# A grouped feed-forward moved into its layer's causal attention, its router behind the first unit, and weights laid out ahead

## The chip, the cores and the metric

One NeuronCore of a Trainium2 chip runs the whole program in one launch. The metric is device time in microseconds (us) of one execution. Two times are close enough to be called the same when they differ by less than about half a per cent.

## The reference

Four layers work on x, 2 sequences of 1024 tokens of 128 channels. In each, the normalized input goes both to an attention and to a feed-forward, and the layer's output joins the two (the feed-forward's result, after an activation, here silu, multiplies the attention's before it is added to the input). The layers: linear attention and a capacity mixture of experts; near (relative) attention and a ternary feed-forward; rotary causal attention and a grouped mixture; biased causal attention and a clamped mixture. Each attention has 16 heads of 8 channels (the first has 64).

The third layer's feed-forward, cut to its core:

```python
scores = sigmoid(x @ w_gate.T)                      # 16 experts, in 4 groups
group_scores = top_k(scores.reshape(T, 4, 4), 2)[0].sum(-1)
allowed = the 2 best groups;  idx = the 4 best experts among them
w = scores[idx] / (scores[idx].sum(-1) + 1e-6)
y = sum over experts of w * ((silu(x @ w1.T) * (x @ w3.T)) @ w2.T)   # F = 64 each
  + the same with the shared expert (F = 128) and no gate
```

All tokens go through all experts and are weighted: 16 experts of 64 rows make 8 blocks of 128, the shared one a ninth. Everything is float32.

## The kernel before

Channels or tokens lie on 128 partitions; the 2048 tokens are 4 chunks of 512. Program parts ("phases") follow one another, each with a block per engine: the prologue of a layer's attention (`a2j`: joins the layer before, normalizes, projects q, k, v), the attention (`a2a`), its output projection (`a2o`), the feed-forward (`f2`). The names of the fourth layer are `a3j`, `a3a`, `a3o` and `f3`.

`causal_attention` (L2149) goes through 8 units, each one sequence and 4 heads. A unit's first pass has 20 jobs ("max"): TensorE writes scores (bf16, split into parts) into one of two "rooms" of 128x1024 in PSUM (L2450, masks L2457), and VectorE takes row maxima from it (L2333). After half of the tokens the maxima are split into three bf16 parts, turned by TensorE (job "maxima", L2462), cast (L2358) and stored by DMA into the stacks as further rows (L2403). The second pass has 40 steps ("st"): scores again, less the maxima, transposed, into one of three PSUM banks (L2481, masks L2488); ScalarE takes exp (L2422); and 12 "pv" steps multiply with the values (L2500, float32). After half of a unit ScalarE copies the result (L2429), and a job "context" turns it in a room (L2469), where VectorE divides it (L2369, L2372).

TensorE takes its work in a list that `work_order` (L2191) writes ahead by a model of costs and due times: at each point the first pass's next job or the second pass's next step, whichever it expects to be able to start sooner. The orders of ScalarE (`act_order`) and of the SyncE DMA queue (`dma_order`) follow from that list. SyncE first loads the next unit's stacks, then the weights of the layer's feed-forward and of the next prologue (`after`), then takes rows and loads in that order, and last stores the gates.

Behind all first passes come the router's jobs, in the same rooms (`GroupRouter`, L1087): four "weight" jobs turn 25 blocks of the feed-forward's weights (L1117) and VectorE copies them out (L1128); logits (L1036); then a chain on VectorE (L1133 to L1164), with one exp on ScalarE (L1045), that chooses groups and experts; two jobs that turn the gates (L1050, copies L1054). While that runs, TensorE has what is left of the second pass.

`grouped_ffn` (L1240) then has 36 steps (4 chunks, 9 blocks): two products 128x512 into PSUM (L1268, L1271), silu (L1295), their product (L1314), that times the gate rows (L1319; two DMAs per step bring a gate row to 64 partitions each), and the down product, which adds up over the 9 blocks (L1282). The shared block has no gate (L1308). ScalarE takes the chunk's silu into `gT` (L1288). Everywhere in it up runs two steps ahead of down.

Of the kernel before, what the change touches and what calls it, by code (L numbers as in the profile page):

```python
# [20 lines left out]
ALU = mybir.AluOpType  # L21
# [3 lines left out]
P = 128  # L25
BATCH = 2
# [183 lines left out]
def linear_weights(nc, ph, w):  # L210
    H, DH, F = 16, 64, 32
    PAIRS = H * DH // P
    wq, wk, wv = (ph.sb(n, [P, H * DH]) for n in ("wq", "wk", "wv"))
# [5 lines left out]
    pairs = [(wq[:], w["Wq"]), (wk[:], w["Wk"]), (bq[:], columns(w["bq"])), (bk[:], columns(w["bk"])),  # L219
# [4 lines left out]
    return (wq, wk, wv, wproj, bq, bk, bv, bproj, featq, featk), pairs  # L224


class Features:
# [5 lines left out]
    def __init__(self, nc, k, ph, tiles, out):  # L233
        self.nc, self.k = nc, k
        self.wq, self.wk, self.bq, self.bk, self.featq, self.featk = [tiles[i] for i in (0, 1, 4, 5, 8, 9)]
        self.wqf, self.wkf, self.bqf, self.bkf = out
        self.wT = [ph.sb(name, [P, self.PAIRS, DIM]) for name in ("wqT", "wkT")]
        self.turn, self.prod = [ph.ps(f"turn{i}") for i in range(2)], [ph.ps(f"prod{i}") for i in range(4)]
        self.key_bias = ph.sb("key_bias", [P, self.PAIRS, self.FP])
        self.turned, self.copied, self.multiplied, self.biased = ph.sem("turned"), ph.sem("copied"), ph.sem("multiplied"), ph.sem("biased")  # L240

    def weights(self, pe):

        lots = [(i, h) for i in range(2) for h in range(2)]
        for n in range(len(lots) + 1):
            if n < len(lots):
                i, h = lots[n]
                if n >= 2:
                    pe.wait_ge(self.copied, n - 1)
                for g in range(4):  # L250
                    mm = self.nc.tensor.transpose(self.turn[n % 2][:, g * P:(g + 1) * P],
                                                  (self.wq, self.wk)[i][:, (4 * h + g) * P:(4 * h + g + 1) * P], self.k.ident[:])
                mm.then_inc(self.turned, 1)
            if n:
                i, h = lots[n - 1]
                pe.wait_ge(self.copied, n)
                for g in range(4 * h, 4 * h + 4):
                    mm = self.nc.tensor.matmul(self.prod[i][:, g * self.FP:(g + 1) * self.FP], self.wT[i][:, g, :],
                                               (self.featq, self.featk)[i][:], start=True, stop=True)
                if h:  # L260
                    mm.then_inc(self.multiplied, 1)
# [801 lines left out]
class GateRows:  # L1063
# [11 lines left out]
    def load(self, sp, m, srcs, hid_ready, read_by):  # L1075

        if m >= self.KEPT:
            sp.wait_ge(hid_ready, read_by)
# [366 lines left out]
H = 16  # L1445
# [1775 lines left out]
```

## Time and profile before

| | us |
|---|---|
| median of 3 runs | 1858.84 (1857.61 to 1865.55) |
| the profiled execution | 1859.92 |
| its span, first to last instruction | 1858.0 |
| TensorE busy | 1544.7 (83%) |
| VectorE busy | 1175.6 (63%) |
| ScalarE busy | 918.5 (49%) |
| GpSimd busy | 478.4 (26%) |
| mean granted TensorE clock | 0.903 |

Where the stages of the third layer lie, in us from the span's start:

| stage | from | to |
|---|---|---|
| prologue a2j | 879 | 931 |
| attention a2a, first passes | 931 | 1156 |
| attention a2a, rest of the second passes | 1156 | 1225.5 |
| projection a2o | 1225.7 | 1233.8 |
| feed-forward f2 | 1234 | 1327.4 |
| fourth layer's prologue a3j | 1327.9 | 1371 |

Engines: PE is TensorE, PEld its weight loads, DVE VectorE, ACT ScalarE, POOL GpSimd, SP SyncE with its DMA queue. PE's ends are modelled, so that consecutive matmuls overlap in their listed durations; a busy TensorE isn't one at its peak. "PEclk" is the clock granted to TensorE as a share of 2.4 GHz. L12 is line 12 of the kernel before.

### The profile page before, as it was taken

The numbers are of one execution on the slowest core, as the hardware profiler recorded it, in microseconds if no ns is written. First come the engines' busy times: TensorE is split into PE (matmuls) and PEld (weight loads), VectorE is DVE, ScalarE is ACT, GpSimd is POOL, SyncE is SP. The second block draws the span as 40 slices with busy tenths as digits, with TensorE's granted clock in tenths as the row PEclk, the third lists the DMA queues.
The fourth block names the chain that finished last, engine by engine and source line by source line (L and its number), as shares of the span: only waits on it lengthen the run. The fifth ranks groups of instructions, "written<-read, shape, count | busy, mean of one in ns | idle before, by whom it ended". The sixth has DMA issues, their size and how long they took to land. (4 is left out here: it accounts for less than half of the span.)

```text
span 1858.0 us, 32947 instructions
## 1 busy us (share of the span) xinstructions
PE 1544.7 (83%) x12129; PEld 746.3 (40%) x12129; DVE 1175.6 (63%) x2514; ACT 918.5 (49%) x1765; POOL 478.4 (26%) x416
## 2 busy tenths in 40 slices
PE   5979745998888888888569988899838988889997
PEld 4656522334343443434224444344323343344443
DVE  4324667755765675805668888435657888617777
ACT  2332232666666666674226666432214666554443
POOL 0702447756766665720300000000020100000000
PEclk9989765999999999999759999689867999889999
DMA  7232257666766766610430100023170010004332
GB/s 213 86 92 72 54 167 196 177 161 163 191 170 163 197 155 167 175 39 9 128 85 19 37 20 19 1 66 91 37 222 16 23 36 19 2 4 104 101 99 82
DMA packets 225671, 179.15 MB, mean 96 GB/s; under 512 B 59536, under 2 KB 194120, under 8 KB 225352
## 3 DMA queue, kind: packets, MB, share of 16 engines
q1 hardware_dynamic: 215400, 160.34, 32.6%
q10 hardware_dynamic: 8064, 12.51, 2.3%
q0 software_dynamic: 2048, 4.20, 0.8%
q8 instruction: 97, 1.59, 0.4%
q14 instruction: 62, 0.51, 0.1%
HBM read 108.64 MB, written 67.64 MB: 95 GB/s over the span
## 5 line engine op out<-in xcount | busy, mean ns | idle before, releaser
L1981 DVE TENSOR_REDUCE a1a_partial<-a1a_room 128x4 f32<-128x1024 f32 x192 | 226.4, 1220 | 30.9 <-PE a1a_room L2046 30.2
L2422 ACT ACTIVATE a3a_probsT<-a3a_st 128x512 f32<-128x512 f32 (+2 forms) x320 | 155.6, 560 | 129.5 <-PE a3a_st L2488 79.2
L2422 ACT ACTIVATE a2a_probsT<-a2a_st 128x512 f32<-128x512 f32 (+2 forms) x320 | 155.5, 560 | 129.5 <-PE a2a_st L2488 77.2
L1940 ACT ACTIVATE a1a_probsT<-a1a_st 128x512 f32<-128x512 f32 (+1 forms) x416 | 204.7, 575 | 11.8 <-PE a1a_st L2079 10.5
L2333 DVE TENSOR_REDUCE a3a_maxima<-a3a_room 128x2 f32<-128x1024 f32 (+3 forms) x160 | 170.1, 1112 | 38.2 <-PE a3a_room L2457 24.9
L2333 DVE TENSOR_REDUCE a2a_maxima<-a2a_room 128x2 f32<-128x1024 f32 (+3 forms) x160 | 170.1, 1112 | 28.4 <-PE a2a_room L2457 19.7
L1845 POOL TENSOR_TENSOR a1a_shifted<-a1a_shifted,a1a_best 128x1024 f32<-128x1024 f32 x64 | 121.8, 1904 | 91.0 <-DVE a1a_best L1987 64.7
L2116 PE MATMUL a1a_ctx<-a1a_probsT,a1a_vpad 128*9 128x512 f32 (+3 forms) x1408 | 139.0, 493 | 0.8
L1977 DVE CUSTOM_DVE_ANT_0 a1a_shifted<-a1a_room,a1a_bands 128x256 f32<-128x256 f32 x256 | 93.3, 421 | 73.3 <-PE a1a_room L2046 65.6
L2046 PE MATMUL a1a_room<-stack 48*128 48x128 bf16 (+1 forms) x1376 | 108.4, 261 | 35.8 <-DVE a1a_partial L1981 19.5
L2079 PE MATMUL a1a_st<-stack 51*128 51x512 bf16 (+3 forms) x576 | 116.3, 314 | 19.9 <-ACT a1a_nearT L1947 6.4
L1943 ACT ACTIVATE a1a_probsT<-a1a_st 128x512 f32<-128x512 f32 x128 | 73.4, 603 | 114.0 <-PE a1a_st L2088 114.0
L2382 POOL COPY a_vpad<-a_values 128x256 f32<-128x256 f32 x16 | 6.3, 401 | 428.0 <-PE a3a_ctx L2500 211.8
L2481 PE MATMUL a3a_st<-stack 51*128 51x512 bf16 (+3 forms) x384 | 87.7, 352 | 18.5 <-DMA stack<-a3a_parts 9.4
L2481 PE MATMUL a2a_st<-stack 51*128 51x512 bf16 (+3 forms) x384 | 89.3, 357 | 14.2 <-ACT a2a_probsT L2422 7.8
L2500 PE MATMUL a3a_ctx<-a3a_probsT,a_vpad 128*32 128x512 f32 (+3 forms) x768 | 90.5, 549 | 7.7 <-ACT a3a_probsT L2422 4.7
L2500 PE MATMUL a2a_ctx<-a2a_probsT,a_vpad 128*32 128x512 f32 (+3 forms) x768 | 92.5, 560 | 4.0 <-ACT a2a_ctxT L2429 2.0
L2046 PEld LDWEIGHTS a1a_room<-stack 48*128 48x128 bf16 x1376 | 46.6, 99 | 117.9 <-DVE a1a_partial L1981 62.1
L2450 PE MATMUL a3a_room<-stack 48*128 48x512 bf16 (+3 forms) x384 | 68.0, 356 | 25.0 <-DMA stack<-k 14.4
L2450 PE MATMUL a2a_room<-stack 48*128 48x512 bf16 (+3 forms) x384 | 67.7, 354 | 25.1 <-PEq L2570 15.9
L1400 ACT ACTIVATE f_below<-f_a,r_r_gate_room 128x512 f32<-128x512 f32 x64 | 44.0, 687 | 85.7 <-PE f_a L1374 85.6
L1857 POOL TENSOR_TENSOR a1a_beyond<-a1a_probsT,c_beyond_mask 128x512 f32<-128x512 f32 x56 | 70.9, 1272 | 56.3 <-ACT a1a_probsT L1943 56.3
(491 smaller groups left out, 3139.0 us busy)
## 6 DMA issues: line engine op xcount, KB each, us to landing
a1a_bands<-a_band SPq DMA_DIRECT2D x112, 192.0 KB, 4.0
a_near<-a1a_shifted SPq DMA_DIRECT2D x112, 192.0 KB, 3.1
a1a_near<-a_near SPq DMA_DIRECT2D x64, 256.0 KB, 4.3
f_rows<-l_gates SPq DMA_DIRECT2D x64, 256.0 KB, 3.1
a_band<-a1a_r_mix SPq DMA_DIRECT2D x64, 254.0 KB, 3.7
stack<-q SPq DMA_DIRECT2D x96, 96.0 KB
f_rows<-l_gates SPq DMA_DIRECT2D x64, 128.0 KB, 3.1
stack<-k SPq DMA_DIRECT2D x32, 96.0 KB
```

Of the source, the lines that this page charges most:

```text
L1845: nc.gpsimd.tensor_tensor(shifted[:, V % 2, t], shifted[:, V % 2, t], best[:, V % 2, :, t:t + 1].broadcast_to([P, HG, NEAR]), ALU.subtract ...
L1940: nc.scalar.activation(dst, src, ACT.Exp).then_inc(exp_done, 1)
L1977: ins = nc.vector.tensor_tensor_reduce(shifted[:, V % 2, t, place, :], src[:, place // 2, place % 2, :], band[i][:, place, :], 1.0, LOWEST ...
L1981: nc.vector.tensor_reduce(partial[:, g % 2, :, 1 + r].rearrange("p (a s) -> p a s", a=2), src, X_AXIS, ALU.max).then_inc(job_free, 1)
L2046: mm = nc.tensor.matmul(dst[:, lo + i * P:lo + (i + count) * P], q, rows_of(sides[edge], place, STACK)[:, c * P:(c + count) * P], start=Tr ...
L2079: mm = nc.tensor.matmul(dst[:, to:to + count * P], rows_of(sides[edge], place + j, ALL_ROWS)[:, c * P:(c + 1) * P], query_rows(q_stack, pl ...
L2116: mm = nc.tensor.matmul(ctx[32 * h:32 * h + DH + 1, lo * P:hi * P], vpad[b][right][:, c, h, :], probsT[:, block_index(V, at) % BLOCK_ROOMS ...
L2333: nc.vector.tensor_reduce(best, scores, X_AXIS, ALU.max).then_inc(job_free, 1)
L2422: nc.scalar.activation(probsT[:, block_at % BLOCK_ROOMS, place:place + heads, lo:], src, ACT.Exp).then_inc(exp_done, 1)
L2450: mm = nc.tensor.matmul(dst[:, end - width:end], query_rows(q_stack, place, STACK, I // HALF_TILES)[:, I % HALF_TILES * P:(I % HALF_TILES ...
L2481: mm = nc.tensor.matmul(dst[:, j * width:(j + 1) * width], rows_of(k_stack, place + j, ALL_ROWS)[:, c * P:(c + 1) * P], query_rows(q_stack ...
L2500: mm = nc.tensor.matmul(ctx[32 * PAIRED[h]:32 * PAIRED[h] + 32, lo:], vpad[b][:, c, PAIRED[h], :], probsT[:, block_at % BLOCK_ROOMS, h, lo ...
```

## The change

The third layer's feed-forward stage is removed. Its 36 steps become jobs inside `causal_attention` (class `GroupedStream`): "up" is a job in a room (gate product in its first half, up product in the second), "down" adds into a PSUM bank `y`, which st gives up (two st banks in the third layer, three in the fourth). ScalarE computes tanh(a/2) instead of silu(a), as a * (tanh(a/2) + 1) is 2 silu(a); the factor 2 goes into the gates' sum, and 0.5 into the shared step. VectorE has two operations per step, GpSimd one. ScalarE copies `y` per chunk; the last silu goes to the end of `project_out`.

The router's jobs are logits and two turns; in the third layer they stand behind the second max job of unit 1 and the maxima after it. The planner places an up six us behind the end of the router's chain (which it takes to be 37 us) at the earliest, never more than three ups ahead of the downs, spread so that 14 of 36 are left when the first passes end. SyncE's list gets the gates' store and the gate rows' loads (four ahead of their use). The fourth layer passes `NoStream` and keeps its router at the end.

On the host, `laid_out` transposes and reshapes weights: the first layer's Wq and Wk, the second and third layers' four projections (one load for four), the ternary weights, all of the grouped feed-forward's (four loads for seven), the clamped ones' two planes and bias. What turned or copied them on the chip is removed: 16 transposes and 4 copies of the first layer, 4 transposes and the copies in each of two prologues (the third layer's keeps a scaling in place), 8 transposes and 2 copies in the ternary feed-forward, the clamped router's 8 GpSimd copies and 2 transposes, and the block that clears a weight tile between `f1` and `a2j`.

The diff, cut to its core:

```diff
 class GroupRouter(TailRouter):
-    WEIGHTS, LOGITS, TURNS = range(0, 4), 4, range(5, 7)
+    LOGITS, TURNS = 0, range(1, 3)
...
-            chain(nc.vector.tensor_scalar(self.red[:], self.red[:], 1e-6, None, ALU.add))
+            chain(nc.vector.tensor_scalar(self.red[:], self.red[:], 1e-6, 2.0, ALU.add, ALU.mult))
...
-def grouped_ffn(nc, k, w, tiles, r):
...
+class GroupedStream:
+    UP_NS, DOWN_NS, ACT_NS, DVE_NS, POOL_NS, LATE = 1800.0, 900.0, 620.0, 1500.0, 1350.0, 14
...
+    def up(self, pe, n, dst):
+        c, j = divmod(n, self.J)
+        x = self.k.xnT[:, c * CHUNK:(c + 1) * CHUNK]
+        self.nc.tensor.matmul(dst[:, 0:CHUNK], self.wide_gate[:, j, :], x, start=True, stop=True).then_inc(self.a_done, 1)
+        return self.nc.tensor.matmul(dst[:, CHUNK:2 * CHUNK], self.wide_up[:, j, :], x, start=True, stop=True)
+    def halve(self, act, n, src, job_free, up_at):
+        act.wait_ge(self.a_done, n + 1)
+        if n >= 2:
+            act.wait_ge(job_free, up_at[n - 2] + 1)
+        self.nc.scalar.activation(self.half[:, n % 2, :], src[:, 0:CHUNK], ACT.Tanh, scale=0.5).then_inc(self.half_ready, 1)
+    def vector(self, dve, n, src, job_free):
...
+            self.rows.wait(dve, m, 2)
+            nc.vector.tensor_tensor(self.mid[:, n % 2, :], b, self.rows.of(m), ALU.mult)
+        dve.wait_ge(self.half_ready, n + 1)
+        nc.vector.scalar_tensor_tensor(out=self.turned[:, n % 2, :], in0=self.half[:, n % 2, :], scalar=1.0, in1=a,
+                                       op0=ALU.add, op1=ALU.mult).then_inc(job_free, 1)
+    def gpsimd(self, pool, n, job_free, up_at):
+        pool.wait_ge(job_free, up_at[n] + 1)
...
+        self.nc.gpsimd.tensor_tensor(self.hid[:, n % 2, :], self.mid[:, n % 2, :], self.turned[:, n % 2, :], ALU.mult).then_inc(self.hid_ready, 1)
+    def down(self, pe, n, y):
...
+        pe.wait_ge(self.hid_ready, n + 1)
+        self.nc.tensor.matmul(y[:], self.wide_down[:, j, :], self.hid[:, n % 2, :], start=(j == 0), stop=(j == self.J - 1)).then_inc(self.hid_used, 1)
...
-    ROOMS, ST_BANKS, BLOCK_ROOMS, HALF_TILES = 2, 3, 3, CHUNK // P
+    ROOMS, ST_BANKS, BLOCK_ROOMS, HALF_TILES = 2, 2 if stream.N else 3, 3, CHUNK // P
...
                 if U and j == 1:
                     jobs.append(("maxima", U - 1, 1))
+                    if U == 1 and stream.N:
+                        jobs += router_jobs
...
+            if ups < stream.N and ups < downs + 3 and chain_done < 1e12 and not any(what == "router" for what, _, _ in jobs[:router.JOBS]):
+                up_at = max(chain_done + 6000.0, read[-ROOMS] + latency)
+                base = seen if base is None else base
...
+            if up_at < 1e12 and not (job and job[0] in ("maxima", "context")):
+                due = job is None or ups * (total - base) <= (seen - base) * (stream.N - stream.LATE)
+                if due or max(now, up_at) + stream.UP_NS < max(now, job_at):
+                    job, job_at = ("up", 0, ups), up_at
...
+        if (what, n) == ("router", router.JOBS - 1):
+            dma_order.append(("store", 0, 0))
+            dma_order += [("gates", 0, m) for m in range(min(GateRows.KEPT, stream.N))]
+        if what == "up":
+            pool_order.append(("hid", 0, n))
+            m = stream.gate_index(n)
+            if m and m + GateRows.KEPT - 1 <= stream.last_gate:
+                dma_order.append(("gates", 0, m + GateRows.KEPT - 1))
...
-def project_out(nc, k, tag, woT, bias=None):
+def project_out(nc, k, tag, woT, bias=None, open_gates=False):
...
+                for c in range(NCH if open_gates else 0):
+                    cs = slice(c * CHUNK, (c + 1) * CHUNK)
+                    nc.scalar.activation(k.gT[:, cs], k.gT[:, cs], ACT.Silu).then_inc(opened, 1)
...
-            causal_attention(nc, k, "a2a", queries, keys, values, vpad.tiles, stack, stacked, stored, after, router)
-            project_out(nc, k, "a2o", woT[:])
-            experts(router)
+            causal_attention(nc, k, "a2a", queries, keys, values, vpad.tiles, stack, stacked, stored, after, router, GroupedStream(nc, k, pr, router))
+            project_out(nc, k, "a2o", wide[:, 3 * DIM:], open_gates=True)
...
-                    pe.wait_ge(rounded, 1)
-                    for i, src in enumerate((w1[:].rearrange("p c d -> p (c d)"), w2[:])):
-                        for c in range(C):
-                            mm = nc.tensor.transpose(w_turn[i][:, c * P:(c + 1) * P], src[:, c * P:(c + 1) * P], k.ident[:])
-                        mm.then_inc(w_turned, 1)
...
-    clear(nc, "f2z", wg)
...
+def laid_out(inputs):
+    w = {name: np.asarray(value) for name, value in inputs.items()}
...
+    for name, each, shared in (("gate", "w1_e", "w1_s"), ("up", "w3_e", "w3_s")):
+        rows = np.concatenate([w.pop("L2_ffn_" + each).reshape(-1, DIM), w.pop("L2_ffn_" + shared)], axis=0)
+        w["L2_ffn_w_" + name] = rows.T.reshape(DIM, -1, P)
...
+    w["L3_ffn_gate_up_bias"] = w["L3_ffn_gate_up_bias"].reshape(experts, P, 2).transpose(1, 2, 0)
```

## Rows read from the trace of the kernel before

**Rows 1.** Busy time by stage: from:to, length, busy us (instructions) per engine, clock, DMA.
```profile
931.00:960.00 29.00, 17.91 (x175) 8.14 (x179) 20.00 (x24) 6.20 (x12) 0.74 (x2) 0.56 0.49 126
960.00:1154.00 194.00, 173.02 (x2116) 76.96 (x2110) 167.58 (x242) 122.26 (x257) 2.55 (x7) 0.96 0.09 23
1154.00:1172.00 18.00, 14.92 (x111) 8.73 (x108) 11.05 (x24) 8.00 (x17) 0.00 (x0) 0.99 0.01 2
1172.00:1206.00 34.00, 30.92 (x202) 10.33 (x200) 15.83 (x126) 17.81 (x39) 0.00 (x0) 0.55 0.00 1
1206.00:1226.00 20.00, 17.49 (x122) 6.72 (x123) 2.97 (x4) 8.49 (x19) 0.00 (x0) 0.66 0.06 8
1226.00:1234.00 8.00, 7.02 (x47) 6.52 (x45) 2.77 (x4) 2.35 (x4) 0.00 (x0) 0.79 0.00 0
1234.00:1328.00 94.00, 92.99 (x217) 41.04 (x218) 46.71 (x68) 24.93 (x42) 0.00 (x0) 1.00 0.32 90
```

**Rows 2.** The same view in shorter stretches: the steady state and the tail.
```profile
1020.00:1050.00 30.00, 27.73 (x351) 12.75 (x350) 26.21 (x39) 20.50 (x44) 0.55 (x2) 1.00 0.10 29
...
1205.00:1215.00 10.00, 9.32 (x44) 2.51 (x42) 0.00 (x0) 5.99 (x12) 0.00 (x0) 0.50 0.01 2
```

**Rows 3.** Groups by line, feed-forward, 1234 to 1328 us: count, busy us, mean ns.
```profile
L1319 DVE TENSOR_TENSOR f_hid<-f_mid,f_rows 128x512 f32<-128x512 f32 x32 | 22.1, 692 | 3.7 <-DMA f_rows<-l_gates 2.4 <-DVE f_mid L1314 0.3
L1314 DVE TENSOR_TENSOR f_mid<-f_b,f_acted 128x512 f32<-128x512 f32 x32 | 22.1, 689 | 36.5 <-PE f_b L1271 36.5
L1295 ACT ACTIVATE f_acted<-f_a 128x512 f32<-128x512 f32 x36 | 21.5, 597 | 65.9 <-PE f_a L1268 65.9
```

**Rows 4.** Single lines elsewhere: durations ns, shortest/median/longest, first and last start.
```profile
L1431 DVE SCALAR_TENSOR_TENSOR f_mid<-f_linear,f_acted x64: 691/692/694, 1680.1 to 1845.4; 128x512 f32<-128x512 f32 x64
...
L1857 POOL TENSOR_TENSOR a1a_beyond<-a1a_probsT,c_beyond_mask x56: 1263/1272/1285, 295.3 to 817.1; 128x512 f32<-128x512 f32 x56
```

**Rows 5.** Groups by line on ScalarE, whole execution: table loads at the exps.
```profile
L2422 ACT ACT_TABLE_LOAD x2 | 2.6, 1283 | 9.1 <-PEq L2570 9.1
```

**Rows 6.** VectorE in order of time around the router: start, us, instruction, idle before.
```profile
1159.03 4.23 DVE L1128 COPY r_r_turned<-a2a_room 128x1024 f32<-128x1024 f32 x4 [0.74 <-PE a2a_room L1117]
1166.54 0.42 DVE L1133 TENSOR_SCALAR r_r_score<-a2a_room 128x256 f32<-128x256 f32 x1 [3.28 <-PE a2a_room L1036]
1169.19 0.29 DVE L1139 TENSOR_SCALAR r_r_score<-r_r_score 128x256 f32<-128x256 f32 x1 [2.22 <-ACT r_r_score L1045]
...
1187.07 0.42 DVE L1164 TENSOR_TENSOR r_r_gates<-r_r_gates,r_r_red 128x256 f32<-128x256 f32 x1
```

**Rows 7.** SyncE's queue in order of time, third and fourth layers' starts.
```profile
943.72 4.05 SPq L90 DMA_DIRECT2D l_w<-in_L_ffn_w_s  x3
948.14 29.79 SPq L2403 DMA_DIRECT2D stack<-a2a_parts  x6
...
1383.50 7.44 SPq L90 DMA_DIRECT2D l_bias<-in_L_ffn_gate_up_bias  x1
```

**Rows 8.** TensorE's waits, third and fourth layers' attention: total us, times, longest.
```profile
PE a2a_st L2481 <- DMA stack<-a2a_parts: 5.5, 1, 5.5
...
PE a3a_st L2481 <- DMA stack<-a3a_parts: 9.4, 1, 9.4
```

**Rows 9.** The page's costliest groups: the third layer's maxima.
```profile
L2333 DVE TENSOR_REDUCE a2a_maxima<-a2a_room 128x2 f32<-128x1024 f32 (+3 forms) x160 | 170.1, 1112 | 28.4 <-PE a2a_room L2457 19.7
```

**Rows 10.** All engines in order of time, at f1's start and after its end.
```profile
842.64 0.76 DVE L873 TENSOR_SCALAR l_w<-l_w 128x512 f32<-128x512 f32 x2
...
843.99 1.04 PE L904 MATMUL f1w_w_turn<-c_ident,l_w 128*128 128x128 f32 x8
...
845.99 1.52 PE L932 MATMUL f_a<-xnT,f_w1T 128*128 128x512 f32 x3 [0.97 <-PEq L858]
...
877.63 0.17 DVE L1331 MEMSET l_wg<- 128x128 f32 x1 [3.20 <-PEq L924]
878.98 0.35 SPq L90 DMA_DIRECT2D l_wide<-in_L_attn_Wq  x1
```

More of the change, by code:

```diff
@@ L2195, in work_order @@
         jobs = []
+        router_jobs = [("router", 0, n) for n in range(router.JOBS)]
         for U in range(UNITS):
@@ L2231, in work_order @@
                         event_at = max(event_at, copied_at + latency)
-            if max(now, event_at) < max(now, job_at):
+            down_at = 1e12
+            if downs < ups:
+                down_at = hid_at[downs] + latency
+                if downs % stream.J == 0:
+                    down_at = max(down_at, y_at + latency)
+            if max(now, down_at) <= min(max(now, event_at), max(now, job_at)):
+                order.append(("down", 0, downs))
+                now = max(now, down_at) + stream.DOWN_NS
+                downs += 1
+                if downs % stream.J == 0:
+                    y_at = act = max(act, now + latency) + 620.0
+            elif max(now, event_at) < max(now, job_at) or job and job[0] == "up" and max(now, event_at) == max(now, job_at):
                 events.pop(0)
@@ L2273, in work_order @@
                     now += 120
[L2274 to L2275 removed]
+                    dve = max(dve, now + latency) + 250
+                    rows_at[U, n] = dve + rows_in_dma
                 else:
@@ L2278, in work_order @@
                     now += 4 * 130
-                    read.append(max(read[-1], now + latency) + 700)
+                    dve = max(dve, now + latency) + 700
+                read.append(dve)
         return order
     order = work_order()
-    jobs = [event for event in order if event[0] in ("max", "maxima", "context", "router")]
+    jobs = [event for event in order if event[0] in ("max", "maxima", "context", "router", "up")]
+    up_at = {n: J for J, (what, _, n) in enumerate(jobs) if what == "up"}
     act_order, owed = [], []
@@ L2295, in causal_attention @@
     act_order += [copy for _, copy in owed]
-    dma_order = []
+    dma_order, pool_order = [], [("pad", U, 0) for U in range(BATCH)]
+    if stream.N:
+        pool_order.append(("router", 0, 0))
     for what, U, n in order:
@@ L2436, in _ @@
                     q_stack, k_stack = stack[U % len(stack)]
-                    if what in ("max", "maxima", "context", "router"):
+                    if what in ("max", "maxima", "context", "router", "up"):
                         dst = room[J % ROOMS]
```

421 lines of the change are left out of this document (195 added, 226 removed).

## The prediction

> **What bounds the kernel now.** I read the busy time by stage first [rows 1]: its row from 1234 to 1328 us is the third layer's feed-forward alone, the five from 931 to 1226 its attention, the one between its output projection. In the feed-forward TensorE is busy 92.99 of 94 us at the full clock, while VectorE has 46.71, ScalarE 24.93 and GpSimd nothing; so this stage is bound by TensorE. In the body of the attention (960 to 1154) TensorE has 173.02 of 194 us and VectorE 167.58: two engines close to full, each waiting in turn for the other. Shorter windows [rows 2] show it in the steady state (27.73 and 26.21 of 30 us), and then the tail, where the second pass runs alone: TensorE 9.32 of 10 us by its records, VectorE nothing, and the granted clock 0.50, the lower of its two levels.
>
> So there is no idle TensorE time into which 93 us could vanish. From 931 to 1328 TensorE is busy 17.91 + 173.02 + 14.92 + 30.92 + 17.49 + 7.02 + 92.99 = 354.3 of 397 us. What merging can win is part of the 42.7 us that are left, and what the low clock costs: 48.4 busy us between 1172 and 1226 at 0.55 and 0.66 would be 28.5 at the full clock (30.92 x 0.55 + 17.49 x 0.66), 19.9 less.
>
> **The work that moves.** Each of 36 steps is three products: 92.99 us / 108 = 0.86 us each, so an up job takes 1.72 and a down job 0.86 us of TensorE. That is not reduced. ScalarE's silu of 597 ns [rows 3] becomes a tanh of the same shape, taken as the same. VectorE's two products, 689 and 692 ns [rows 3], become one product and one scalar_tensor_tensor; that form took 692 ns [rows 4], so 1.38 us stay. One product more goes to GpSimd, which took 1272 ns for that shape [rows 4]; 36 of them are 46 us on an engine busy 3.3 us in the attention, hence hidden as long as a down job comes 1.3 us or more behind the up's reader. The final silu stays four 128x512 passes but moves behind the projection's copies: 4 x 0.6 = 2.4 us, of which the copies' own waits can hide little; I take +2.4 (bounds 0 and +3.7, with a table load of 1.28 [rows 5] on the path, which takes the place of the old stage's own).
>
> VectorE's sum shows that it doesn't become the bound: 217 us in the attention, less 4.2 for the weight copies that go [rows 6], plus 36 x 1.38 = 50, is 263 us in a stage of some 365.
>
> **The terms,** against the stretch 931 to 1328.
> 1. Weight jobs gone. VectorE's four copies take 4.23 us from 1159.03, and the logits' result is read at 1166.54 [rows 6]. TensorE worked at the second pass beside them, so the saving is what 25 transposes take of TensorE: bounds 0 and -4.2, taken at -3.
> 2. Start. SP issues seven weight loads up to 948.14 before the first attention rows; the last three take 4.05 us, and TensorE's second pass then stands 5.5 us [rows 7, 8]. Four loads replace the seven. By the rows a load takes 0.7 to 1.35 us of SP: 2.8 to 5.4 instead of 7. So -1.6 to -4.2, taken at -3, all of it while the stall is longer than that.
> 3. Router. Its exponential's result is 2.65 us behind the logits, its chain ends at 1187.49: 21 us from 1166.54 [rows 6]. Now it stands in unit 1, where VectorE's maxima are stopped for this time. The first pass is late by about 28 us (21, logits and turns). TensorE meanwhile has unit 0's second pass, so it doesn't stand; but that is the mix that ran at 0.50 in the tail. The low clock took 19.9 us there in 54 us (1172 to 1226), so some 8 in a stretch of 21; they are counted in term 4. In the old place the chain delayed only the projection, not the maxima.
> 4. Clock. The tail now has 14 of 36 steps, 36 us of the products which ran at 1.00 in the old stage. Bounds: 0 and -19.9. I take -20 for the tail, as the row of the old feed-forward is the nearest to its work, and +8 for the router's stretch: -12.
> 5. Idle time in the attention. TensorE's 21.0 of 194 us and 8.7 in the tail. In 960 to 1154 run some 7 of the 8 units, 27 to 28 us each, with some 24 on each of TensorE and VectorE (170.1 / 8 = 21.3 us of VectorE's are maxima [rows 9]). With 22 steps in the first pass, 3.2 per unit still to come, TensorE gets 8 and VectorE 4.4 more: TensorE is then the bound and VectorE has slack, so the waits for a room should shrink. Against that, st has two banks for three, an up holds one of two rooms through tanh and two VectorE operations (1.72 + 0.86 + 0.7, some 3.3 us, in which a max job could have used it), and each down waits for GpSimd. Bounds: -25 (nearly all idle time filled) and +25 (0.7 us lost per step). I take -10.
> 6. The stage's own fill and the step between stages: 1 us idle before 1328 and one change of program: -1. With the silu's +2.4 the stage gives -3 -3 -12 -10 -1 +2.4 = -26.6.
>
> **Weights laid out elsewhere.** In the second layer's feed-forward the rounding ends at 843.40 (842.64 + 0.76) and the main loop starts at 845.99 [rows 10]: transposes and copies between are gone, a change of program of about 1 us stays: -1.6 (0 to -2.6). The clearing of a gate tile costs from 877.63 to 878.98 [rows 10] a program of its own: -1.2 (0 to -1.35). In the fourth layer the rows wait behind a bias load whose issue stood 7.44 us, and TensorE for 9.4 us [rows 7, 8]; the load is now contiguous, but a 2 MB load ahead of it stays: 0 to -7, taken at -1. The fourth router's GpSimd copies lie beside the attention, which it waits for nowhere. The transposes of the first layer's weights and of the second and third layers' projections run beside VectorE's normalization and router chain, which end later: taken at 0; 8 transposes took 1.04 us [rows 10], so the 16 of the first layer bound it at -2.1.
>
> Sum: -26.6 - 1.6 - 1.2 - 1 = -30.4. The profiled execution took 1859.92 us (span 1858.0), 1.1 above the median; from there 1829.5, or **1828 us** against the median.
>
> **A rule that speaks against it.** In the start's stall, TensorE had 5.5 us with other work in its list and did none of it, as the second pass's matmul at the head waited for rows [rows 8]. The Trainium skill states that as a rule (PSUM — Partial Sum Buffer, Engine vs sequencer instructions): matmuls start and complete in program order. The trace agrees with its 5.5 us, and by the rule every misjudged place in the written order is a stall, which is the second rival.
>
> **Rivals.**
> A. Better: the ups fill nearly all gaps and the clock is full throughout. Terms 4 and 5 become -20 and -25: 1859.9 - 53 = about 1805. For it: TensorE's 99% in the old feed-forward. Against: 27.73 of 30 us in the best window of the attention [rows 2].
> B. Given back: the order written out fits the chip badly. The planner counts 37 us for the chain and spreads the ups from there; the trace has 21. Each stall of 0.7 us per step makes term 5 +15 instead of -10: about 1854, no measurable change. If the ups were not placed in the first pass as it says, all 36 would stand in the tail, where nothing but 28 us of second pass overlaps: the same result.
> C. Slower: the clock stays at 0.50 in the tail. Nothing but second pass runs at the router and much of it in the tail; if the 14 steps don't bring the clock up, their 36 us become 72, and the tail's gain of 20 is lost: -30 + 20 + 36 = +26, 1886. At the clock of 0.66 that the tail's last row shows, the steps cost 18 more and the rest keeps about 10 of the gain: -30 + 10 + 18 = -2. So it decides below about 0.65. Against it: the old stage held 1.00 with the same products; for it: 0.50 at 9.32 of 10 us busy.
> D. Slower: tanh and exp exchange ScalarE's tables. A load took 1.283 us [rows 5]; 36 x 2 of them are 92 us of ScalarE, whose sum goes from 163 + 24 to 279 of some 365. Each pair of 2.6 us outlasts what two st banks hold, by about 1.5: 36 x 1.5 = +54, 1883. No tanh is in the trace; ScalarE's exps of the two causal layers went with one load each [rows 5].
> The Trainium skill (ScalarE: Activation LUTs, Table sets: the hidden batching unit) puts exp and tanh into one set, which would mean no load between them; no run here shows it, and it is why D gets little.
>
> **Chances.** Forecast (1812 to 1843) 0.52; A 0.15; B (1843 to 1866) 0.18; C 0.10; D 0.05. A measurement of this kernel tells a change from none at about 0.5%, 9.3 us: 1849.5 to 1868.1. A third of B lies below it: faster 0.52 + 0.15 + 0.06 = 0.73; same 0.12 of B and 0.01 of C's near side: 0.13; slower 0.14. The range 1798 to 1866 leaves out 0.04 of A and 0.13 of C and D. The forecast's own is 1812 to 1843.
>
> **What would show it.** Terms 1 and 2: first rows issued near 945 us, no stall of 5 us behind them. Term 3: maxima stopped for some 28 us near 960, TensorE busy meanwhile, its clock low. Term 4: the granted clock in the stage's last 60 us; 0.9 or more bears me out, 0.6 is C. Term 5: TensorE's busy share from 990 to the first pass's end, above 0.92 for me, below 0.85 for B, and its waits for hid and for exps. D: table loads beyond one in the attention. The projection should begin near 1287, the fourth layer near 1300. I'm wrong if the fourth layer begins after 1318, or if the gain comes from elsewhere than the third layer.

## The result: slower by 2.3%

The changed kernel takes 1903.7 us (median of 4 runs, 1898.3 to 1908.9), the kernel before 1859.4 in the same session: ratio 1.023 (1.019 to 1.027). The forecast was 1828. The profiled execution took 1898.3 (span 1896.4, TensorE busy 1564.3, mean granted clock 0.892) beside 1859.9 (1858.0, 1544.7, 0.903).

Where the third layer's stages begin, in us of the span:

| | before | after |
|---|---|---|
| prologue a2j | 879.0 | 875.9 |
| attention a2a | 931.2 | 930.0 |
| last of the first passes ends | 1154.3 | 1264.3 |
| projection a2o | 1225.7 | 1357.8 |
| fourth layer a3j | 1328.0 | 1367.8 |
| end | 1858.0 | 1896.4 |

From a2a to a3j 396.8 us became 437.8, 41.0 more. Ahead of it 1.2 us are won (3.1, of which the prologue gives back 1.9), behind it 1.6. These small sums are not told from chance: the 15 profiles of this kernel and of the experiments below, which have the same code up to a2a, begin a2j between 873.8 and 883.0 us. Only the longer prologue is in all of them (54.0 to 54.5 us, before 52.2). So the loss lies in one stage. Busy time by stretch of that stage after the change (from:to, length, busy us and instructions of PE, PEld, DVE, ACT, POOL; granted clock, DMA share, GB/s), which answers to [rows 1]:

```profile
930.00:960.00 30.00, 20.59 (x203) 9.36 (x205) 22.53 (x27) 7.15 (x13) 0.88 (x3) 0.57 0.44 122
960.00:1061.00 101.00, 75.81 (x476) 32.14 (x470) 60.04 (x195) 29.42 (x57) 5.45 (x5) 0.72 0.12 30
1061.00:1264.00 203.00, 186.95 (x1794) 78.47 (x1795) 154.63 (x220) 114.55 (x223) 24.65 (x23) 1.00 0.13 38
1264.00:1358.00 94.00, 83.69 (x443) 30.23 (x440) 23.34 (x44) 45.39 (x86) 17.76 (x14) 0.89 0.09 26
1358.00:1368.00 10.00, 7.37 (x51) 6.82 (x50) 2.77 (x4) 6.10 (x10) 0.00 (x0) 0.83 0.01 2
```

The second row is the one to look at. Before, 960 to 1154 ran at 0.96 with TensorE busy 89% [rows 1]; now 101 us run at 0.72 with 75%. Behind it the clock is 1.00 with 92%. Shorter stretches, which answer to [rows 2]: steady state, steps in the tail, the tail's last us.

```profile
1100.00:1130.00 30.00, 28.24 (x242) 11.66 (x243) 22.73 (x35) 17.34 (x33) 4.13 (x4) 1.00 0.12 36
...
1310.00:1325.00 15.00, 15.00 (x79) 5.96 (x77) 4.84 (x8) 6.55 (x13) 3.81 (x3) 1.00 0.00 1
1345.00:1355.00 10.00, 8.75 (x74) 3.49 (x74) 0.00 (x0) 4.68 (x10) 0.00 (x0) 0.50 0.00 0
```

**A balance of TensorE.** Stage = work + clock + idle. From the trace of each kernel I sum the time from each product's start to the next product's start or its own end, whichever is sooner; half of what ran at 0.50 is "clock" (what the full clock would have saved), the rest is "work", and the gaps are "idle". A few us are missing where records are.

| a2a to a3j | length | work | clock | idle |
|---|---|---|---|---|
| before | 396.8 | 318.3 | 35.3 | 41.6 |
| after | 437.8 | 330.0 | 43.9 | 61.0 |
| difference | +41.0 | +11.7 | +8.6 | +19.4 |
| of it in the first 150 us | | -32.9 (work not yet done) | +19.4 | +11.7 |

So by 150 us into the stage the changed kernel is some 32 us behind, by work not done. Later it does 27.3 us of work per 30 (150 to 330 us; before 26.8 from 60 to 240), but has 11.7 more to do; in the tail the clock costs 9.3 where it cost 20.8.

**The stop.** VectorE in order of time after the change (start, us, instruction, idle before and what ended it), which answers to [rows 6]:

```profile
962.36 0.27 DVE L2367 CAST a2a_parts<-a2a_room 48x128 bf16<-48x128 f32 x1
969.62 0.42 DVE L1093 TENSOR_SCALAR r_r_score<-a2a_room 128x256 f32<-128x256 f32 x1 [6.99 <-PE a2a_room L1009]
971.66 0.29 DVE L1099 TENSOR_SCALAR r_r_score<-r_r_score 128x256 f32<-128x256 f32 x1 [1.61 <-ACT r_r_score L1018]
...
989.54 0.42 DVE L1124 TENSOR_TENSOR r_r_gates<-r_r_gates,r_r_red 128x256 f32<-128x256 f32 x1
...
998.00 0.26 DVE L2381 RECIPROCAL a2a_inv<-a2a_room 128x16 f32<-128x16 f32 x1 [7.31 <-PE a2a_room L2500]
...
998.88 2.34 DVE L1027 COPY r_r_gateT<-a2a_room 16x1024 f32<-16x1024 f32 x2 [0.29 <-PE a2a_room L1023]
1007.40 0.69 DVE L1246 TENSOR_TENSOR s<-a2a_room,xn_one 128x512 f32<-128x512 f32 x1 [6.18 <-DMA xn_one<-l_gates]
...
1008.60 3.06 DVE L2342 TENSOR_REDUCE a2a_maxima<-a2a_room 128x2 f32<-128x768 f32 x3
```

No maximum is taken from 962.6 to 1008.6: 46 us. The chain has 20.3 of them, 969.6 to 990.0, with 1.6 for the exponential; three waits have 20.5: 7.0 for the logits (at half clock), 7.3 for the last context of unit 0, behind which TensorE's list has the turns of the gates, and 6.2 for the first gate row, which goes out to memory and comes back. Contexts, copies and the first step's products are the other 5. TensorE in the same stretch:

```profile
995.03 1.51 PE L2531 MATMUL a2a_ctx<-a2a_probsT,a_vpad 128*32 128x256 f32 x16
997.34 0.63 PE L2500 MATMUL a2a_room<-c_ident,a2a_ctxT 128*128 128x128 f32 x4 [0.80 <-ACT a2a_ctxT L2456]
997.80 1.91 PE L1023 MATMUL a2a_room<-c_ident,r_r_gates 128*16 128x128 f32 x16
1000.14 1.13 PE L1226 MATMUL a2a_room<-xnT,l_wide_gate 128*128 128x512 f32 x2 [0.43 <-DVE r_r_gateT L1027]
...
1008.74 0.50 PE L2477 MATMUL a2a_room<-stack 48*128 48x384 bf16 x2 [6.26 <-DVE r_turned L1248]
```

It did use unit 0's second pass as cover, for the most part at half clock (0.61 from 962 to 997), and at 996.5 that was used up. Unit 1's second pass can't start, for its rows need maxima that VectorE has not taken. So the pipeline between the passes runs empty and has to be filled again, at the low clock: 0.56 from 1005 to 1020.

**Changes of product.** The same three products in the old stage and (second fence) in the new one's stretch from 1061 to 1342 us, by line (count, busy us, mean ns, idle before):

```profile
L1268 PE MATMUL f_a<-xnT,r_r_turned 128*128 128x512 f32 x72 | 36.8, 593 | 1.0 <-PEq L2783 1.0
L1271 PE MATMUL f_b<-xnT,r_r_turned 128*128 128x512 f32 x72 | 36.8, 592 | 0.0
L1282 PE MATMUL f_y<-f_hid,r_r_turned 128*128 128x512 f32 x72 | 36.4, 592 | 0.0
```
```profile
L1226 PE MATMUL a2a_room<-xnT,l_wide_gate 128*128 128x512 f32 x62 | 35.8, 661 | 0.1
L1262 PE MATMUL a2a_y<-s,l_wide_down 128*128 128x512 f32 x64 | 35.1, 630 | 0.0
L1227 PE MATMUL a2a_room<-xnT,l_wide_up 128*128 128x512 f32 x63 | 33.3, 610 | 0.0
```

Each product has two records here (72 for 36 steps), and a listed duration holds part of the next record's too (592 ns listed where 429 lie between two starts). By starts, the first record of a run behind a product of another kind has 533 ns to the next start, the last one before another kind 525, one inside a run 429. That is 0.1 us per change and about four changes per step (into and out of an up, into and out of a down); ups and downs took 92.4 us of work before and 104.9 after.

**Small terms.** SyncE after (start, us, instruction), then TensorE's waits (us in total, times, longest), for [rows 7] and [rows 8]:

```profile
941.68 0.43 SPq L90 DMA_DIRECT2D l_wide_down<-in_L_ffn_w_down  x1
942.16 21.94 SPq L2418 DMA_DIRECT2D stack<-a2a_parts  x4
```
```profile
PE a2a_st L2512 <- DMA stack<-a2a_parts: 3.7, 1, 3.7
...
PE a3a_st L2512 <- DMA stack<-a3a_parts: 7.3, 1, 7.3
```

Rows issued 6.0 us sooner, the stall 1.8 shorter. Groups on ScalarE in the stage (count, busy us, mean ns), for [rows 5]:

```profile
L1234 ACT ACTIVATE r_half<-a2a_room 128x512 f32<-128x512 f32 x36 | 21.5, 598 | 41.8 <-PE a2a_room L1226 41.7
...
L2445 ACT ACT_TABLE_LOAD x1 | 1.3, 1283 | 3.4 <-PEq L2599 3.4
L2838 ACT ACT_TABLE_LOAD x1 | 1.3, 1283 | 0.0
```

36 tanh among 320 exps with one load, that of the first exp; the last silu brings its own. The Trainium skill (ScalarE: Activation LUTs, Table sets: the hidden batching unit), which puts the two into one set, is borne out here.

### The profile page after: what moved, and what is told of

Same layout as the page of the kernel before. It is cut to its first block and busy times, and to the rows that moved or that the text cites. A ratio compares the mean times of both kernels' runs of the same rounds, so it can differ in the third digit from the quotient of the medians.

```text
span 1896.4 us, 32805 instructions
## 1 busy us (share of the span) xinstructions
PE 1564.3 (82%) x12067; PEld 739.7 (39%) x12067; DVE 1167.9 (62%) x2513; ACT 927.7 (49%) x1759; POOL 518.7 (27%) x444
## 5 line engine op out<-in xcount | busy, mean ns | idle before, releaser
L2445 ACT ACTIVATE a2a_probsT<-a2a_st 128x512 f32<-128x512 f32 (+2 forms) x320 | 164.5, 553 | 185.0 <-PE a2a_st L2519 111.9
L1887 ACT ACTIVATE a1a_probsT<-a1a_st 128x512 f32<-128x512 f32 (+1 forms) x416 | 204.7, 575 | 13.0 <-PE a1a_st L2026 11.7
L1993 PE MATMUL a1a_room<-stack 48*128 48x128 bf16 (+1 forms) x1376 | 106.7, 259 | 37.4 <-DVE a1a_partial L1928 19.3
L1255 POOL TENSOR_TENSOR s<-s,r_turned 128x512 f32<-128x512 f32 x36 | 45.6, 1267 | 283.0 <-DVE r_turned L1248 283.0
L2512 PE MATMUL a2a_st<-stack 51*128 51x512 bf16 (+3 forms) x384 | 94.4, 355 | 20.4 <-ACT a2a_probsT L2445 15.6
```

The lines of the kernel that those rows point to most:

```text
L1887: nc.scalar.activation(dst, src, ACT.Exp).then_inc(exp_done, 1)
L1993: mm = nc.tensor.matmul(dst[:, lo + i * P:lo + (i + count) * P], q, rows_of(sides[edge], place, STACK)[:, c * P:(c + count) * P], start=Tr ...
L2445: nc.scalar.activation(probsT[:, block_at % BLOCK_ROOMS, place:place + heads, lo:], src, ACT.Exp).then_inc(exp_done, 1)
L2512: mm = nc.tensor.matmul(dst[:, j * width:(j + 1) * width], rows_of(k_stack, place + j, ALL_ROWS)[:, c * P:(c + 1) * P], query_rows(q_stack ...
```

## The experiments

Ratios are to the kernel before, which had 1860 to 1862 us in these sessions. Theory 1 was that the stopped maxima are what costs.

**The layout alone.** The changed host layout with the old feed-forward stage and the router at the end.

```diff
-            causal_attention(nc, k, "a2a", queries, keys, values, vpad.tiles, stack, stacked, stored, after, router, GroupedStream(nc, k, pr, router))
-            project_out(nc, k, "a2o", wide[:, 3 * DIM:], open_gates=True)
...
-          (rotary_weights, rotary_attention, grouped_weights, None),
+          (rotary_weights, rotary_attention, grouped_weights, grouped_ffn),
```

> Only the second part of the change: weights laid out ahead and no weight jobs, but the third layer's feed-forward is again a stage of its own, its router behind the first passes and three st banks. Both theories: the changed kernel's other stages gave 1.2 us net ahead of the attention (prologue 3.1 us sooner, itself 1.9 us longer) and 1.6 us behind it, and 3.7 us of TensorE for the weight jobs go. So 3 to 7 us faster than before, 1852 to 1856 us.

Measured 1854.8, ratio 0.996 (0.994 to 0.999). The new layout with the weight jobs gone wins about 7 us; the merged feed-forward costs 49 (1903.7 - 1854.8). Windows of the attention's first passes, its tail, the feed-forward, and the stretch that answers to 960 to 1061 above:

```profile
933.00:1148.00 215.00, 185.03 (x2205) 82.67 (x2206) 186.51 (x263) 122.25 (x252) 3.13 (x9) 0.92 0.13 37
1148.00:1221.00 73.00, 63.61 (x489) 25.34 (x482) 25.63 (x150) 41.37 (x86) 0.15 (x1) 0.74 0.02 3
1222.00:1324.00 102.00, 100.01 (x266) 47.65 (x266) 49.59 (x72) 27.51 (x46) 0.00 (x0) 0.99 0.32 83
...
963.00:1064.00 101.00, 89.54 (x1058) 39.22 (x1058) 88.06 (x127) 59.87 (x124) 1.34 (x4) 0.93 0.09 26
```

**The router at the end.** All 36 steps then stand behind the first passes.

```diff
-                    if U == 1 and stream.N:
-                        jobs += router_jobs
...
-        jobs += [] if stream.N else router_jobs
+        jobs += router_jobs
```

> The changed kernel with one thing undone: the router's jobs stand behind all first passes, as before, so that all 36 steps come in the tail. Theory 1 (the early router drains the pipeline: it stops the first pass for 46 us, and up to 1061 us TensorE does 64 us of work in 131, where the kernel before needed some 97): the first passes end near 1156 again, the stage is 30 to 40 us shorter, 1858 to 1870 us. Theory 2 (the steps themselves cost it, through rooms shared with the maxima, two st banks and changes between kinds of product, wherever they stand): 5 to 15 us less at most, 1885 to 1895 us.

Measured 1902.9, ratio 1.022 (1.017 to 1.028): nothing gained though the maxima stop nowhere. Theory 1 in its simple form fell with that. The windows show why it doesn't answer the question:

```profile
930.00:1179.00 249.00, 207.75 (x2176) 88.46 (x2172) 188.86 (x263) 127.64 (x250) 2.88 (x8) 0.82 0.12 32
1179.00:1362.00 183.00, 166.01 (x735) 68.60 (x731) 71.98 (x222) 67.68 (x128) 46.06 (x37) 0.85 0.17 47
```

The same first passes take 249 us where they took 215. What differs in them is the third st bank, given to `y`, and the order that is written for two banks. TensorE's waits for exps, there and (second fence) in the layout alone:

```profile
PE a2a_st L2510 <- ACT a2a_probsT L2443: 18.7, 38, 0.7
```
```profile
PE a2a_st L2596 <- ACT a2a_probsT L2529: 4.7, 15, 0.5
```

So two costs can stand for each other: a stop with two banks, or two banks without steps to fill the gaps.

**The chain in slices.** The router stays in unit 1, but its chain is cut into 9 slices, one before each of the next maxima (`choose_gates` is the same chain with a yield between the parts), and the gates' turns come behind the unit's 15th job instead of its second.

```diff
+            self.slices = self.choose_gates(dve)
...
-                        jobs += router_jobs
+                        jobs += router_jobs[:1]
+                if U == 1 and j == 14 and stream.N:
+                    jobs += router_jobs[1:]
...
+                            if 1 < waited:
+                                next(router.slices, None)
```

> The changed kernel with the router's logits where they are, but the chain on VectorE cut into 9 pieces, each behind one of the next maxima of unit 1, and the two turns 12 jobs later, so that the first pass goes on. Theory 1: TensorE keeps first-pass work beside the second pass, the gap in the maxima goes, VectorE is the bound for 20 us: 10 to 25 us faster than the changed kernel, 1875 to 1890 us. Theory 2: no difference beyond 5 us, 1895 to 1905 us.

Measured 1883.2, ratio 1.013 (1.008 to 1.018): 20 us back, as theory 1 says.

**The chain cut short.** This kernel leaves out the choice of groups and experts: gates are the squared scores, normalized. The planner is told 8 us for the chain in place of 37.

```diff
-            pairs = score[:].rearrange("p t (g a b) -> p t g a b", g=G, a=2)
...
-            chosen = sum_hot(nc, chain, hot, self.K)
-            chain(nc.vector.tensor_tensor(gates[:], chosen, score[:], ALU.mult))
+            chain(nc.vector.tensor_tensor(gates[:], score[:], score[:], ALU.mult))
```

> The changed kernel with the router's choice of groups and experts left out (the gates are the squared scores, normalized, for all experts), and the planner told 8 us for the chain. About 16 of 20 us of the chain on VectorE go. Theory 1: the first pass starts again 20 to 28 us sooner, the stage gains 15 to 25 us: 1875 to 1888 us. Theory 2: at most 5 us, as VectorE isn't the bound of the stage: 1893 to 1903 us.

Measured 1885.3, ratio 1.013 (1.008 to 1.018): 18 us back by another way. Maxima stop for 30 us, from 966.9 to 996.6, where they stopped for 46; of what is left, 19.4 us are waits for the logits, the turned gates and the first gate row:

```profile
996.58 3.18 DVE L2323 TENSOR_REDUCE a2a_maxima<-a2a_room 128x2 f32<-128x768 f32 x3
```

The stretch that answers to 960 to 1061, in the sliced and (second fence) the short one:

```profile
961.00:1062.00 101.00, 80.16 (x606) 35.91 (x606) 71.09 (x208) 37.56 (x74) 5.46 (x5) 0.81 0.12 31
```
```profile
963.00:1064.00 101.00, 85.75 (x630) 36.54 (x628) 61.19 (x90) 38.17 (x74) 7.97 (x7) 0.81 0.14 37
```

Busy time times clock is 64.9 and 69.5, where the changed kernel has 54.6 and the layout alone 83.3. Both win what theory 1 gives, in the place that it names, and both stay short of the undisturbed stretch.

**Only the planner's estimate.** 21 us for the chain, as measured, in place of 37.

```diff
-    PE_NS, DVE_NS, CHAIN_NS = [3800.0] + 2 * [1800.0], [500.0] + 2 * [1300.0], [37000.0] + 2 * [0.0]
+    PE_NS, DVE_NS, CHAIN_NS = [3800.0] + 2 * [1800.0], [500.0] + 2 * [1300.0], [21000.0] + 2 * [0.0]
```

> The changed kernel with one number changed: the planner takes the chain to be 21 us, not 37. If the wrong estimate is a large part of the 46 us that the maxima stand (turns wait behind all of unit 0's second pass, 7 us after the chain's end): 5 to 15 us faster than the changed kernel, 1888 to 1898 us. If the stop itself is what costs, whatever the estimate: within 5 us, 1898 to 1909 us.

Measured 1906.9, ratio 1.026 (1.023 to 1.029): nothing. With the better estimate the maxima still stop for 43 us, from 962.5 to 1005.6, so the estimate makes 3 of the 46. A stop of nearly the same length costs the same: the estimate isn't the cause.

```profile
1005.61 1.82 DVE L2342 TENSOR_REDUCE a2a_maxima<-a2a_room 128x2 f32<-128x768 f32 x2 [0.28 <-PE a2a_room L2484]
```

**What two banks cost without steps.** The layout alone, with two st banks in both causal attentions; and with three banks but the order written as for two.

```diff
-    ROOMS, ST_BANKS, BLOCK_ROOMS, HALF_TILES = 2, 2 if stream.N else 3, 3, CHUNK // P
+    ROOMS, ST_BANKS, BLOCK_ROOMS, HALF_TILES = 2, 2, 3, CHUNK // P
```
```diff
-                    event_at = max(exps[-ST_BANKS] + latency, ...)
+                    event_at = max(exps[-2] + latency, ...)
```

> layout_alone (the feed-forward a stage of its own, weights laid out ahead: 1854.8 us) with one thing changed: two st banks instead of three in the third and fourth layers' attention. Theory A (the bank that y takes is dear while no step fills the gaps: in router_last the first passes took 249 us for the same work as layout_alone's 215, 25 us of it by the low clock): 25 to 35 us per attention, two of them: 1895 to 1925 us; the granted clock dips within the first passes. Theory B (two banks suffice, as exps waited only 5 us for a bank; router_last was late for another reason): below 1865 us.

> layout_alone with the planner told that it has two st banks, so that the order is the one of layout_two_banks, while the chip has three. Theory A1 (the missing bank on the chip costs the 107 us: TensorE stands behind an exp and its clock falls): 1855 to 1880 us. Theory A2 (the order that is written for two banks is bad by itself, holding back the second pass): 1925 us or more.

Measured 1962.0, ratio 1.056 (1.051 to 1.061), and 1925.0, ratio 1.033 (1.029 to 1.037). 107 us in two attentions is far more than expected; 70 of them come from the written order alone, with all three banks there, and 37 more when the third bank is missing on the chip too. Both ways TensorE meets gaps: in the third layer the waits for exps are 27.6 us with two banks (7.9 in the layout alone), and with the order alone it waits for rooms instead, 19.3 us (8.8). First fence: two banks; second: the order.

```profile
PE a2a_st L2596 <- ACT a2a_probsT L2529: 27.6, 52, 0.7
```
```profile
PE a2a_room L2561 <- DVE a2a_maxima L2426: 19.3, 40, 0.9
```

In the first of them the tail ran at 0.61 of the clock (0.74 in the layout alone):

```profile
1180.00:1273.00 93.00, 76.20 (x515) 30.08 (x511) 25.68 (x150) 43.85 (x88) 0.40 (x1) 0.61 0.02 2
```

**Three banks until the steps begin.** The router at the end, and `y` takes the third bank only when the first down comes; then the same with 21 us for the chain; then with all three banks kept, the nine downs of a chunk in one run into the context's bank between two halves.

```diff
-        y = ph.ps("y") if stream.N else None
+        y = st[2] if stream.N else None
...
-                    event_at = max(exps[-ST_BANKS] + latency, ...)
+                    event_at = max(exps[-(2 if downs else ST_BANKS)] + latency, ...)
```
```diff
-        y = st[2] if stream.N else None
+        y = ctx if stream.N else None
...
-                order.append(("down", 0, downs))
+                order += [("down", 0, n) for n in range(downs, downs + stream.J)]
```

> router_last with three st banks until the first down; y takes the third bank from there (all steps are in the tail). Theory A: the first passes end near 1150 again instead of 1179, 25 to 33 us faster than router_last: 1868 to 1878 us, still slower than layout_alone, since the chain has only second pass beside it, and the steps then nothing to fill. Theory B: as router_last, 1895 to 1907 us.

> last_three with the planner told 21 us for the chain instead of 37, as the traces have it. If the order's wrong estimate costs it (turns and first steps placed 16 us behind what they could be, the second pass used up before them at the low clock): 8 to 16 us faster than last_three, 1855 to 1868 us. If not: within 4 us of it.

> last_three_21 with the bursts of sliced_burst, so three st banks in the tail too. Only some 30 us of second pass stand beside steps there: 0 to 8 us faster than last_three_21, 1848 to 1856 us, by theory A. If banks don't matter where steps fill the gaps: 1854 to 1860 us, the bursts costing as much as they save.

Measured 1867.0 (ratio 1.003, 1.001 to 1.005), 1855.8 (0.997, 0.995 to 1.000) and 1851.5 (0.995, 0.993 to 0.997). So the third bank, with the order written for it, was worth 36 us, and the estimate 11 in this place, where the early place gave nothing for it. First passes and the rest of the stage, in the last of them:

```profile
935.00:1148.00 213.00, 183.67 (x2202) 82.11 (x2199) 186.30 (x263) 121.99 (x252) 3.10 (x9) 0.92 0.13 38
1148.00:1313.00 165.00, 154.71 (x707) 63.69 (x702) 72.09 (x222) 65.12 (x126) 46.08 (x37) 0.92 0.19 52
```

The first passes are those of the layout alone again, and the 36 steps lie beside the second pass. This version lies below both kernels; its interval and that of the layout alone overlap, so that those two aren't told apart.

**The bank and the changes in the early place.** The sliced chain with that run of downs and three banks; and with each down joined to an up.

```diff
-    ROOMS, ST_BANKS, BLOCK_ROOMS, HALF_TILES = 2, 2 if stream.N else 3, 3, CHUNK // P
+    ROOMS, ST_BANKS, BLOCK_ROOMS, HALF_TILES = 2, 3, 3, CHUNK // P
```
```diff
-            if downs < ups:
+            joined = not pair and job is not None and job[0] == "up" and ups - downs >= 2
+            if downs < ups and (ups == stream.N or joined):
```

> chain_sliced with three st banks throughout: y has no bank of its own, GpSimd's results are kept for 9 steps, and the 9 downs of a chunk run in one burst into the pv bank, between two halves of a unit. Theory A (two banks and the changes of product are what chain_sliced still pays): ups and downs 98 us instead of 104, TensorE's idle time back from 52 to some 42, 10 to 20 us faster than chain_sliced, 1863 to 1873 us, still not faster than layout_alone. Rival (the rest is the chain and 50 us of VectorE in the first passes): 1879 us or more.

> chain_sliced with each down placed directly ahead of the up two steps later, so that TensorE goes over to these products and back once per step, not twice. Theory 3 (each change costs 0.1 us: the first product of a run began its successor after 533 ns and the last after 525, against 429 in the old stage): ups and downs take 97 us of TensorE instead of 104, 5 to 9 us faster than chain_sliced, 1874 to 1878 us. Rival (the products are slower inside the attention wherever they stand, or the down that is held back costs as much again): 104 us and 1883 us or more.

Measured 1878.6, ratio 1.010 (1.007 to 1.012), and 1910.1, ratio 1.028 (1.022 to 1.033). With steps in the first pass the third bank and the run of downs together gave some 5 us; the run also keeps nine results waiting, so the bank's part alone is not shown. Joining lowered the work of ups and downs from 104.3 to 99.0 us, and lost 23 in clock and idle time: the price of a change is real, but it is cheaper than work in the wrong place.

**What is left of the sliced chain's loss.** Two more of it: without the choice (gates as in the short chain, 2 slices, turns behind the 8th job); and with the first up 14 us behind the chain in place of 6.

```diff
-                if U == 1 and j == 14 and stream.N:
+                if U == 1 and j == 7 and stream.N:
```
```diff
-                up_at = max(chain_done + 6000.0, read[-ROOMS] + latency)
+                up_at = max(chain_done + 14000.0, read[-ROOMS] + latency)
```

> Left out: the choice of groups and experts; the gates are the squared scores, normalized. Otherwise the kernel with the chain cut into slices, now with 2 slices in place of 9, and the turned gates 7 max jobs behind the logits. Theory 1 (what is left of the loss is VectorE's work of the chain, some 18 us, which has moved from the tail, where VectorE was idle, into the stretch where it is full): 10 to 15 us less than the sliced chain's 1883, that is 1868 to 1873. Rival (the loss that is left is changes of product and places of the steps that the written order misjudges): 1879 or more.

> The sliced chain with its first step placed 14 us behind the end of the chain in the planner's time, where it was 6. Theory: the 6.2 us for which VectorE's first product stood waiting for the first gate row go, and TensorE's idle time behind them: 1876 to 1879 against 1883. Rival: the later start only pushes steps together further on, and the row is off the path: no change, 1880 to 1886.

Measured 1888.0, ratio 1.014 (1.011 to 1.018), and 1883.6, ratio 1.012 (1.008 to 1.017): both missed. The first says that VectorE's work of the chain is not what is left: the early stretch did improve, busy 87.61 at 0.85, which is 74.5 at the full clock after 64.9, but later stretches gave it back, 10 us of it by the clock (behind the first 150 us of the stage the balance has 19.0 of "clock", in the sliced chain 9.0). In the second the wait for the gate row is 6.2 us, where it was 6.7, because the first step did not move: its first VectorE operation starts 84 us behind the start of the stage, in the sliced chain 85. So it says nothing on that wait's price.

```profile
965.00:1066.00 101.00, 87.61 (x677) 38.39 (x677) 66.14 (x98) 40.99 (x79) 7.93 (x7) 0.85 0.14 37
```

## Why the prediction was wrong

**Term 3 failed, and with it the sign.** It had the place right (maxima stopped, TensorE with unit 0's second pass at a low clock) and the price wrong: "late by about 28 us", "it doesn't stand", +8. The stop is 46 us. Left out were the wait for unit 0's last context, behind which the gates' turns stand in TensorE's list, and the way of the gate row through memory; the logits at half clock took 7. And the cover has an end: once unit 0's second pass was used up, TensorE had neither rows for unit 1 nor rooms, and the pipeline had to be filled anew. Some 32 us of the stage's 41 are lost in its first 150 us. The runs bear out the stop as the cause of about 20 (slices, and the short chain); the estimate is none of it. In the sum of the stage, -26.6 forecast and +41.0 measured, the terms that were off are idle time (-10, measured +19.4), the clock (-12, +8.6) and work (-3, +11.7).

**Term 5 had the wrong sign.** Forecast -10, bounds -25 to +25; measured +19.4, of which 11.7 in the first 150 us. In the steady state TensorE was indeed fuller (28.24 of 30, against 27.73 in [rows 2]), but part of that is the price of changes. From 990 to the end of the first passes its share is 0.87, between the 0.92 that I gave for me and the 0.85 for B. The waits for a room, which were to shrink, grew (first line before, second after), and VectorE did not become free to help: in order, it stood 64.9 us before the steps' first operation, waiting for the up.

```profile
PE a2a_room L2450 <- DVE a2a_maxima L2333: 8.3, 18, 0.8
PE a2a_room L2477 <- DVE a2a_maxima L2342: 12.3, 24, 0.9
DVE s L1246 <- PE a2a_room L1227: 64.9, 30, 4.0
```

**A term was missing.** I took the 108 products at 0.86 us in any place. Between products of another kind they cost 12 us more (92.4 and 104.9 us of work).

**Term 4.** The steps did bring the clock up: 1.00 at 1310 to 1325, and 0.89 over the last 60 us before the projection (1298 to 1358), where I had asked for 0.9. The tail's loss fell from 20.8 to 9.3, so -11.5 where I had -20; no step is left from 1338 on, and from 1342 to 1354 it ran at 0.50. Rival C is refuted. The router's share of it was +19.4 against +8.

**What held.** The layout, by the terms that it holds (1, 2, f1w, f2z, fourth layer) forecast at -9.8, measured at -7. By their own rows f1w and f2z give 3.0 where 2.8 was forecast: the gap before the second layer's main loop went from 2.6 to 1.1 us, the one before a2j from 1.75 to 0.3; a longer prologue, which the sum did not have, took about 2 of it back. Rows issued at 942.2, where "near 945" was named (1.2 of the 6.0 us lie in the earlier start of the stage); the stall shrank to 3.7 and did not vanish, and the fourth layer's to 7.3 from 9.4. Rival D is refuted by the one table load. GpSimd's product took 1.27 us as taken:

```profile
L1255 POOL TENSOR_TENSOR s<-s,r_turned 128x512 f32<-128x512 f32 x36 | 45.6, 1267 | 283.0 <-DVE r_turned L1248 283.0
```

Rival B named the planner's 37 us and +15 for term 5; that term came to +19.4, but by another cause, as the estimate alone gave nothing back. My mark for being wrong, a fourth layer later than 1318, was met: 1367.8.

**Left open.** The sliced chain is still 21 us above the kernel before and 28 above its own layout. By the balance of the two traces (29.6 us of the stage) that is 15.6 more work, some 12 of it in ups and downs, 12.4 more idle time and 1.6 of clock; the first 150 us are some 20 behind those of before. Of the idle time 7.2 us are one stop, behind the steps' first VectorE operation, which waits for the gate row:

```profile
1017.69 0.61 PE L2517 MATMUL a2a_room<-stack 48*128 48x512 bf16 x2 [7.18 <-DVE r_turned L1270]
```

No run takes this stop away, so that it costs as much as it lasts is not shown; leaving out the chain's own work gave nothing, and the third bank with the run of downs some 5 us.

## What to carry to other kernels

A wait hidden by another unit's work is hidden only as long as that work lasts: compare the length of the whole stop, with everything queued on the in-order engine and every trip through memory in it, to what the cover holds, and add the refill of the pipeline behind it. Work that fills a bound engine's gaps must bring more than it costs in changes and buffers: here the same steps, behind the first passes and with all banks kept, left the time of the layout alone as it was; beside the first passes, with the early router and two banks, they added 49 us to it.

## What was not expected of the hardware

- A float32 128x512 product costs about 0.1 us more at each change from and to the attention's products (533 and 525 ns to the next start, against 429 inside a run). Most of its neighbours were bf16; beside the float32 products with the values it was the same, 533 and 522; ahead of a float32 turn of a context (three cases) there was none, 430.
- One PSUM bank out of three for the transposed scores: 107 us in two attentions (1854.8 to 1962.0), 70 of them by the written order alone. The waits that grew are not all of it: in the third layer's tail TensorE's busy share went from 0.87 to 0.82 and the granted clock from 0.74 to 0.61. That the gaps brought the clock down is read from these two rows, not tested.
